# Sorted feed-forward of one layer: every tile of gathered rows and of results has its own place, and all gathers are issued ahead of all scatters

## The reference, cut to what matters

```
def _L0_ffn_ref(x, gate_w, gate_b, w1, b1, w2, b2, wg, bg, w3, b3):
    def _expert_ffn(x, w1, b1, w2, b2, wg, bg, w3, b3):
        x1 = jnp.einsum('bsh,hf->bsf', x, w1) + b1
        x2 = jnp.einsum('bsh,hf->bsf', x, w2) + b2
        z = x1 * x2
        s = jax.nn.silu(jnp.einsum('bsf,fg->bsg', z, wg) + bg)
        return jnp.einsum('bsg,gh->bsh', s, w3) + b3
    logits = jnp.einsum('bsh,he->bse', x, gate_w) + gate_b
    topv, topi = jax.lax.top_k(logits, TOPK)          # 2 of 8 experts for each row
    probs = jax.nn.softmax(topv, axis=-1)
    out = jnp.zeros_like(x)
    for e in range(E):
        we = jnp.sum(probs * (topi == e), axis=-1)
        out = out + we[..., None] * _expert_ffn(x, w1[e], b1[e], w2[e], b2[e], wg[e], bg[e], w3[e], b3[e])
    return out
...
x = x + jnp.tanh(g_ffn[0]) * _L0_ffn_ref(_layernorm(x, axis=-1), ...)
```

## Time and profile before

| what | value |
|---|---|
| median of 3 runs | 1141.05 us (1138.16 to 1146.92) |
| the profiled execution | 1142.24 us, its span 1140.5 us |
| mean granted clock of TensorE | 0.842 |
| the block loop, first to last `last_product` | from 97 to 221 us of the span |

### The profile page before, as it was taken

The page is one execution under the profiler, slowest core; times in us unless marked ns, Lnnn a source line. Parts: engine busy times, 40 slices in busy tenths (PEclk is TensorE's granted clock), DMA queues, the critical chain, the costliest instruction groups (busy, mean ns, idle before and its releaser), DMA issues.

```text
span 1140.5 us, 14655 instructions
## 1 busy us (share of the span) xinstructions
PE 823.3 (72%) x5027; PEld 558.8 (49%) x5027; DVE 676.7 (59%) x1850; ACT 358.5 (31%) x725; POOL 353.5 (31%) x464
## 2 busy tenths in 40 slices
PE   2718887827787777777529379479989897995484
PEld 1716766613443443344229347346734475774363
DVE  5681122276666667763887856867547545896521
ACT  1213333214355554434100233145420032452210
POOL 5423556443202211301743800210200101544154
PEclk9757989957999999998759579879889897998588
DMA  8415455320000000000000000000000022001221
GB/s 239 158 42 157 148 152 154 90 53 1 1 1 1 2 1 1 1 1 1 0 1 1 0 1 1 1 0 1 2 0 1 0 73 75 1 1 50 71 65 31
DMA packets 50844, 45.00 MB, mean 39 GB/s; under 512 B 6756, under 2 KB 46715, under 8 KB 50515
## 3 DMA queue, kind: packets, MB, share of 16 engines
q1 hardware_dynamic: 46994, 36.45, 10.8%
q0 software_dynamic: 3776, 7.61, 2.5%
HBM read 36.90 MB, written 7.80 MB: 39 GB/s over the span
## 4 chain that ended last, share of the span: by engine, by line
PE 55%; DVE 31%; issue 6%; POOL 2%; DMA 2%; ACT 2%; another core or an unknown queue 0%; SPq 0%; POOLq 0%; DVEq 0%; ACTq 0%
DVE scratch L1516 7%; PE psum L2219 5%; PE psum L1065 4%; PE psum L1849 3%; PE psum L1303 3%; DVE XN L152 3%; DVE stats L141 2%; PE psum L2409 2%; PE psum L1323 2%; PE psum L1877 2%; PE psum L1868 2%; PE psum L2439 2%; PE psum L557 2%; DVE scratch L1707 2%; PE psum L1048 2%
## 5 line engine op out<-in xcount | busy, mean ns | idle before, releaser
L193 POOL TENSOR_SCALAR veps<-moments 128x4 f32<-128x4 f32 x44 | 8.5, 194 | 334.5 <-DVE moments L144 334.0
L1516 DVE TENSOR_REDUCE scratch<-psum 128x2 f32<-128x640 f32 x128 | 99.2, 815 | 4.5 <-PE psum L1272 4.3
L229 PE MATMUL psum<-ident,XN 128*128 128x128 f32 x144 | 34.4, 389 | 84.5 <-DVE XN L152 68.5
L1272 PE MATMUL psum<-scratch 128*128 128x320 bf16 x256 | 57.9, 317 | 33.8 <-DVE scratch L1516 29.4
L854 DVE SCALAR_TENSOR_TENSOR scratch<-psum,b_block_bias,scratch 128x256 f32<-128x256 f32 (+1 forms) x48 | 18.6, 430 | 100.9 <-PE psum L1054 33.0
L229 PEld LDWEIGHTS psum<-ident,XN 128*128 128x128 f32 x144 | 23.7, 200 | 92.3 <-DVE XN L152 64.6
L240 ACT ACTIVATE XT<-psum 128x512 f32<-128x512 f32 x36 | 21.2, 597 | 133.0 <-PE psum L229 132.9
L2219 PE MATMUL psum<-late,scratch 128*128 128x512 f32 x128 | 58.0, 615 | 5.7 <-DVE routing_wide L2162 5.0
L1065 PE MATMUL psum<-scratch,arena 128*128 128x256 f32 (+1 forms) x192 | 49.1, 407 | 14.0 <-DVE scratch L854 10.1
L2343 POOL TENSOR_TENSOR scratch<-scratch,arena 128x1024 f32<-128x1024 f32 x16 | 30.4, 1901 | 91.8 <-DVE arena L2563 91.8
L926 POOL DMA_INDIRECT pair_results<-scratch,b_scatter_at x39 | 39.1, 1003 | 54.6 <-DVE scratch L863 46.7
(11 more groups left out here) (426 smaller groups left out, 2115.2 us busy)
## 6 DMA issues: line engine op xcount, KB each, us to landing
arena<-in_L_ffn_w SPq DMA_DIRECT2D x72, 128.0 KB
arena<-in_L_ffn_wg SPq DMA_DIRECT2D x24, 256.0 KB
wide<-in_L_xattn_Wkv SPq DMA_DIRECT2D x1, 2048.0 KB
arena<-pair_results SPq DMA_DIRECT2D x8, 256.0 KB
wide<-in_L_ffn_W SPq DMA_DIRECT2D x1, 2048.0 KB, 8.7
late<-in_L_ffn_W SPq DMA_DIRECT2D x8, 256.0 KB, 6.9
X<-in_x SPq DMA_DIRECT2D x2, 512.0 KB, 4.8
C<-in_ctx SPq DMA_DIRECT2D x2, 512.0 KB, 6.6
```

The source lines that it names most:

```text
L229: last = t.transpose(c.bank[self.banks[g % 2]][:, i * P:(i + 1) * P], self.src[:, GROUP * g + i, :], c.ident[:])
L1272: last = t.matmul(bank[2 + 2 * (n % 2) + q][:, 0:self.KEYS], self.QT[:, 4 * g + pair, i * P:(i + 1) * P], self.KM[:, h + q, :], start=True ...
L1516: v.tensor_reduce(self.top[:, i, h:h + 2], c.psum[:, k:k + 2, 0:self.KEYS], AX.X, ALU.max, negate=True).then_inc(s["maxed"], 1)
```

## The change

Every one of the 39 tiles gets its own place, for its gathered rows and for its results. The gathered rows lie in `c.XT` (tiles 0 to 15), in `c.XN` (16 to 31) and in `scratch` (32 to 38); both of the first two are free at this point, since `XN` has been stored to HBM and `XT` was read by the router. The results lie in the arena, one after another. With that the queue of GpSimd is written in another order: all 39 gathers, and then all 39 scatters. A gather of block n now waits for the landing of the gathers of block n - 4 (they count on the same semaphore) in place of `turned`. `take` waits for `result` alone. Numbers of instructions and of DMAs stay as they were.

```diff
@@ class SortedPairStage
-    AHEAD = 3
...
+        ar.take((self.TILES - 2 * NT) * D)
+        self.outs = c.arena_tensor[:, R * 1280:R * 1280 + self.TILES * D]
...
-        self.rows = sc.take(R * self.SLOTS).rearrange("p (u i d) -> p u i d", u=R, i=2)
+        more = sc.take((self.TILES - 2 * NT) * D)
+        homes = (c.XT[:, :], c.XN[:, :, :].rearrange("p j d -> p (j d)"), more)
+        self.rows = [homes[k // NT][:, k % NT * D:(k % NT + 1) * D] for k in range(self.TILES)]
...
-        self.outs = sc.take(R * self.SLOTS).rearrange("p (u i d) -> p u i d", u=R, i=2)
@@ dve
         def take(n):
-            u = n % self.RING
+            at, width = self.tile(n), self.width(n)
             v.wait_ge(s["result"], n + 1)
-            if n >= self.RING:
-                v.wait_ge(self.scattered[u], self.moved(u, n))
-            v.tensor_copy(self.outs[:, u, 0:self.width(n), :].rearrange("p i d -> p (i d)"),
-                          c.bank[7][:, 0:self.width(n) * P]).then_inc(s["out"], 1)
+            v.tensor_copy(self.outs[:, at * D:(at + width) * D], c.bank[7][:, 0:width * D]).then_inc(s["out"], 1)
@@ pool
         def gather(n):
             u = n % self.RING
             if n >= self.RING:
-                g.wait_ge(s["turned"], n - self.RING + 1)
+                g.wait_ge(self.gathered[u], self.moved(u, n))
             for i in range(self.width(n)):
                 at = self.tile(n) + i
-                g.indirect_dma_start(self.rows[:, u, i, :], None, self.given,
+                g.indirect_dma_start(self.rows[at], None, self.given,
...
-                                     self.outs[:, u, i, :], None, bounds_check=2 * NT * P - 1, oob_is_err=False) \
+                                     self.outs[:, at * D:(at + 1) * D], None, bounds_check=2 * NT * P - 1, oob_is_err=False) \
...
-        for n in range(self.AHEAD):
+        for n in range(self.BLOCKS):
             gather(n)
         self.routed.wait(g, "scatter_ready")
         for n in range(self.BLOCKS):
-            if n + self.AHEAD < self.BLOCKS:
-                gather(n + self.AHEAD)
             scatter(n)
@@ pe, turn
-                last = t.transpose(c.bank[6][:, i * P:(i + 1) * P], self.rows[:, u, i, :], c.ident[:])
+                last = t.transpose(c.bank[6][:, i * P:(i + 1) * P], self.rows[self.tile(n) + i], c.ident[:])
```

## The result

The changed kernel took 1151.67 us (median; 1151.37 to 1153.13) beside 1141.84 for the kernel before: ratio 1.0086, 95% interval 1.0045 to 1.0126. So it is 0.9% slower, 30 us above the forecast of 1122, and 3 us above its range (1116 to 1149). Its profiled execution took 1151.75 us. Three of the four runs of the kernel before (1138.16, 1141.05 and 1146.92) are those that were taken ahead of the prediction; the fourth took 1142.63.

What follows compares the result with a forecast made beforehand. TensorE was taken to bound the block loop, GpSimd's queue second. The profiled 1142.2 us less 19 for late signals (7.4 and 14.0 won, some 2.4 left; other terms 0) gave 1123, stated as 1122 us; range 1116 to 1149.

Steps and rivals of the forecast that it cites:

- the late signals: Block loop: TensorE's signals arriving late cost 21.4 us over five steps; taken as nearly all gone, -19 us, chance 0.42.
- A single punctual pair of rows: Last stage: product ends at 1088.67, VectorE starts at 1088.71, 9 us into eight gathers; taken as nearest evidence for gathers alone.
- The forecast for the first 60 us: Gather phase of the loop: late signals of three steps taken as gone, 14.0 us gained, less some 2.4 us remaining.
- the five steps that were costed: Block loop, single block's result to next pair's: 46.9 us where 5 x 5.1 = 25.5 would do, 21.4 us lost.
- The gathers' arithmetic: GpSimd's queue: from 78.15 us, the first gather and 38 more at 1.33 us end at 130.3 us.
- Behind the run: Loop from about 163 us on: GpSimd pauses between scatters, two late steps become punctual, 7.4 us won.
- one unbroken run: Rival, chance 0.13: gathers harm like mixed runs, no pause from 78 to about 150 us, 8.7 us per block; 1148 to 1159 us.
- The backlog of scatters until 163 us: GpSimd's queue: some 13 tiles, 17 us of issue, wait at 130.3 us; caught up at about 163 us, costing 0.
- The rival's mark: Sign for the half or slower case: in the gather phase VectorE or ScalarE start microseconds behind the ends of TensorE's products.
- The second gain: Loop's transposes: late gathered rows cost TensorE 2.1 us, removed from the third block on, counted inside the 21.4 us.
- hidden work of TensorE: Rival no effect, chance 0.23: the 4 us before VectorE starts could be TensorE's own unreported work; 1142 us, within 4.
- queues served in turn: DMA engines in the loop: gathers take their share from weight loads up to 130 us; room for it at 139 GB/s.

Runs made afterwards that it cites:

- e11: Changed kernel, loop started after all rows landed, with added phases of gathers (full rows, 32-byte rows, full rows without weight loads) and memsets beside TensorE: 1255.78 us.
- the late trace: Kernel before, unedited, its profiled execution ahead of the change: 1142.2 us, last result at 221.3 us.
- e6: Kernel before, not edited, run again for its trace in a later comparison: 1119.96 us in its one run.
- e5: Changed kernel, not edited, run again in a later comparison: 1114.75 us, ratio 0.9961 to the kernel before.
- e12: Loop started after all rows landed, with added phases of 12 further full-row gathers as singles, pairs and fours, weights loaded as ever: 1204.68 us.
- e13: Changed kernel's places, but gathers eight blocks ahead of the scatters, then in turn: 1143.75 us, kernel before 1141.10.
- e17: Changed kernel reordered: 15 tiles gathered ahead, then one or two behind each block's scatters: 1137.80 us, ratio 0.9950 to the kernel before.
- e1: Changed kernel's places for every tile, but the DMA order of the kernel before: 1118.88 us, ratio 0.9993 to the kernel before.
- e4: Changed kernel with 38 memsets of about 1.1 us on GpSimd between the gathers of block 3 and block 4: 1144.94 us.
- e8: Changed kernel's places, but gathers eight blocks ahead of the scatters, then in turn: 1115.14 us, ratio 0.9968 to the kernel before.
- e9: Changed kernel's places, order of the kernel before, each gather fetching 32-byte rows in place of 512: 1121.41 us, kernel before 1119.45.
- e10: Changed kernel's places, order of the kernel before, weights loaded for the first four blocks only: 1113.75 us, kernel before 1119.45.
- e14: Changed kernel reordered: 15 tiles gathered ahead, then one or two behind each block's scatters: 1114.38 us, ratio 0.9938 to the kernel before.
- e16: Changed kernel, not edited, run again in a later comparison: 1115.38 us, ratio 0.9956 to the kernel before.
- e7: Changed kernel with each gather fetching rows of 32 bytes in place of 512: 1118.59 us.
- e2: Changed kernel, but the gathers of each block wait until those of the block before have landed: 1160.69 us.

## Why the prediction was wrong

**The step that failed** is the one on the late signals: "That is nearer than the mixed runs, so I take the late signals of the first 60 us as gone too". A single punctual pair of rows, 9 us into a run of eight gathers, was laid above five episodes in runs of six or seven. That row does not speak against harm in a longer run: the changed kernel has the same punctual pair in that stage (1095.83 to 1095.87), and in its own run of 39 gathers signals were punctual for 12 us and late afterwards. Nor does the 9 us count: in e11 signals are late from 4.0 us on. TensorE waits for rows when that run begins and sends only four signals in the whole of it, in both kernels; the punctual one is the third. In the loop the first late one is the fifth to ninth. The forecast for the first 60 us, 14.0 us gained less 2.4, is the term that this row carried; there 38.4 us were lost. The text named this weak place, but for the wrong reason (no weight loads beside it); in e11 signals are late without weight loads too.

**What was right.** *The price of the late signals*: they were costed at 21.4 us, and the kernel before takes 1119 to 1122 us where they are absent and 1141 to 1148 where they are present. The forecast of 1122 is the time of the kernel before without them. That the two agree so well is partly luck: from the late trace to e6 the loop shortens by 22.3 us, but the five steps that were costed give 18.1 of it (46.9 to 28.8, not 25.5, as rows are then waited for), and steps that were counted as sound give the rest. *The gathers' arithmetic*: 130.3 us for their end, measured 128.98; the wait for landings free; transposes waiting only at the start. *Behind the run*: punctual signals, steps of 5.1 us from a single block to a pair, clock 1.00; more was won there (29.5 us, from 144 us on) than the 7.4 counted.

**Sizes.** The rival "one unbroken run" gave 1148 to 1159 with a chance of 0.13, and this is what happened, but with other terms. It took 8.7 us for each block in the run; measured were 38.4 us lost on the first three results, since lateness is not a price per block: it grows with the run, to 34 us. Against that the pace behind it was 4.08 us and not 4.4. The backlog of scatters until 163 us never arose in this run, while in e5 the row of DMAs ended at 162.2. The rival's mark, signals microseconds late in the gather phase, was the one seen. Its time was right by luck: the measured 1151.67 lies in its range because a larger loss ahead was met by a larger gain behind.

**The second gain.** Rows that come late were put at 2.1 us. With punctual signals they are 10.1, because TensorE then arrives earlier; this is the part of the change that works, and it gives 0.4% where nothing holds up the signals.

On what the Trainium skill states in "Perfetto Trace Analysis" (section Tensor Engine Instruction), that TensorE's reported end is computed: read as hidden work of TensorE it would make the late signals part of the program. e5 against the first comparison speaks against that, the same instructions being taken 0.04 us behind their ends in one and up to 34 us in the other, and e11 does so in one trace, where signals are late beside gathers alone. On queues served in turn (the Trainium skill, "DMA: Bandwidth & Descriptors", section SWDGE vs HWDGE vs iDMA): no run here shows how the queues are served, but e5 agrees that there was room, weights and gathers moving 207 GB/s together while TensorE waited for no DMA.

**Open.** Why signals are late in some comparisons (the first, e11, e12 with e13, e17) and not in others (e1 to e4, e5 to e8, e9 with e10, e14 to e16). Within one comparison all runs were of one kind, as far as their times and traces show. The experiments of e1 to e4, e7, e9 and e10 met punctual signals alone, so that in the late kind a pause after each block (e2) and longer memsets (e4) stay untried. The records number the chips but not the machines: number 15 stands once on either side. So the chip, its neighbours and the time are all possible. Where the signal is held up, in TensorE, on its way or at the waiting engine, no row shows, nor whether the issue of the DMAs or their landing holds it up. Signals of VectorE to TensorE were taken within 0.06 us in the midst of it (in the changed kernel 110.29 + 0.88 = 111.17, and TensorE at 111.22).

## What to carry to other kernels

A fix that collects one engine's DMA issues into a single long row removes waits for data and can add waits for signals. Ask of any long row who else must be heard while it lasts. Here singles and pairs with pauses between them were clean, and the order that tried to keep to three at a time won 0.5%. When a few punctual or late pairs decide a forecast, compare how long the run has lasted and how many signals have gone before them in it, and don't rest the forecast on one pair. And measure such a change in more than one comparison: the changed kernel was 0.9% slower in the one with late signals in which it ran, and 0.4% faster in two with punctual ones (e5 and e16).

## What the runs showed of the hardware

- In four of eight comparisons, signals of TensorE reached VectorE, ScalarE and SyncE late, by up to 34 us, while GpSimd issued indirect DMAs at one per 1.3 us. In the other four none did, also where the kernel was the same ("remote" starts: 1 to 21 in each of the six traces of the one kind, none in the thirteen of the other). The kernel before took 1141 to 1148 us in the one kind and 1119 to 1122 in the other.
- Where it exists, rows of 32 bytes show it (8.4 us), and so do full rows without weight loads beside them (10.6 us); ten memsets in a row don't. The first signal late by about 1 us or more is TensorE's fifth to ninth within the run, 3 to 17 us into it. Lateness grows with the run, and the last late signals come up to 4 us behind its end (in the changed kernel one more, at 136.26, 2.1 us behind two scatters).
- Singles 2.7 us apart and pairs with pauses of 2.3 us and more left TensorE 31.86 of 33 us busy; one of three fours cost 1.3 us.
- In the same late stretches, VectorE's signals to TensorE were taken within 0.06 us.
